# Layer 1's attention heads: in each step the last head's context tile stands in front of this head's scores instead of behind them

## The reference

```python
q = _rope((x @ Wq).reshape(N, t, H, DQ).transpose(0, 2, 1, 3))   # H = 16
k = _rope((x @ Wk).reshape(N, t, G, DQ).transpose(0, 2, 1, 3))   # G = 4, each used by 4 heads
scores = (q @ k.T + alibi) / sqrt(DQ)
scores = 30.0 * tanh(scores / 30.0)
probs = softmax(where(causal, scores, -inf))
ctx = probs @ v
out = ctx.reshape(N, t, H * DV) @ Wo + bo
```

## Time and profile before

| | us |
|---|---|
| three timed runs | 852.80, 853.99, 854.36 |
| their median | 853.99 |
| profiled execution | 852.75 |
| its span, first to last instruction | 850.9 |
| PE busy | 783.5 (92% of the span) |
| DVE busy | 609.0 (72%) |
| ACT busy | 465.7 (55%) |
| POOL busy | 422.4 (50%) |

### The profile page before, as it was taken

One profiled execution on the slowest core, in us unless ns is written; L12 is line 12 of the kernel. 1 busy time (PEld: TensorE's weight loads), 2 busy tenths in 40 slices (PEclk: granted clock), 3 DMA queues, 4 the chain that ended last, 5 costly groups with the idle time before them and its releaser, 6 DMA issues.

```text
span 850.9 us, 13950 instructions
## 1 busy us (share of the span) xinstructions
PE 783.5 (92%) x4871; PEld 637.8 (75%) x4871; DVE 609.0 (72%) x1077; ACT 465.7 (55%) x822; POOL 422.4 (50%) x479
## 2 busy tenths in 40 slices
PE   7999999978788878899998999999999997989996
PEld 6776776754233257698998989989999997978884
DVE  7588868457999867878788877997777543445455
ACT  4433342278888733686855565556665724555431
POOL 1767827333555445456444534576656514555530
PEclk9999999997999899999999999999999999999999
DMA  5211194000000040000000000010101599444107
GB/s 183 75 38 37 38 304 126 1 1 1 1 1 2 1 127 27 25 7 25 7 19 7 27 7 7 26 44 32 39 32 46 210 244 382 132 124 112 46 11 237
DMA packets 50115, 59.81 MB, mean 70 GB/s; under 512 B 13559, under 2 KB 41084, under 8 KB 50048
## 3 DMA queue, kind: packets, MB, share of 16 engines
q1 hardware_dynamic: 45488, 50.49, 19.2%
q0 software_dynamic: 4560, 8.44, 2.8%
HBM read 41.11 MB, written 21.86 MB: 74 GB/s over the span
## 4 chain that ended last, share of the span: by engine, by line
PE 58%; DVE 8%; POOL 6%; ACT 6%; issue 4%; DMA 3%; POOLq 0%; ACTq 0%; DVEq 0%; SPq 0%
PE ps L786 12%; PE ps L516 9%; PE ps L518 8%; PE ps L517 8%; PE ps L879 4%; PE ps L876 3%; PE ps L910 3%; POOL A L1777 2%; DMA xa<-xg_scratch 2%; PE ps L613 2%; PE ps L698 2%; PE ps L558 2%; PE ps L858 1%; DVE cap L1477 1%; PE ps L795 1%
## 5 line engine op out<-in xcount | busy, mean ns | idle before, releaser
L786 PE MATMUL ps<-V,P 128*128 128x129 f32 x1152 | 150.7, 276 | 0.0
L1131 ACT ACTIVATE cap<-cap 128x1024 f32<-128x1024 f32 (+7 forms) x128 | 87.1, 680 | 110.3 <-DVE cap L1477 106.6
L786 PEld LDWEIGHTS ps<-V,P 128*128 128x128 f32 x1152 | 143.3, 192 | 2.7
L1477 DVE SCALAR_TENSOR_TENSOR cap<-dist,ps 128x1024 f32<-128x1024 f32 (+7 forms) x128 | 95.3, 750 | 28.7 <-PE ps L518 20.8
L1701 POOL TENSOR_SCALAR_AFFINE_SELECT P<-P 128x128 f32<-128x128 f32 x128 | 38.3, 299 | 143.7 <-ACT P L1136 143.3
L1833 POOL DMA_INDIRECT y_scratch<-y_sb,aux_s x63 | 62.1, 985 | 70.8 <-ACT y_sb L1176 40.3
L1136 ACT ACTIVATE P<-cap 128x1024 f32<-128x1024 f32 (+7 forms) x128 | 87.6, 685 | 4.1
L516 PE MATMUL ps<-q_hi,k_hi 128*128 128x512 f32 x192 | 71.8, 374 | 6.4 <-DVE cap L1477 5.0
L518 PE MATMUL ps<-q_lo,k_hi 128*128 128x512 f32 x192 | 67.0, 349 | 0.0
L517 PE MATMUL ps<-q_hi,k_lo 128*128 128x512 f32 x192 | 66.7, 347 | 0.0
L1629 DVE TENSOR_SCALAR gu<-ps 128x256 f32<-128x256 f32 (+1 forms) x63 | 28.9, 458 | 47.6 <-PE ps L876 16.8
(11 more groups left out here) (288 smaller groups left out, 2104.7 us busy)
## 6 DMA issues: line engine op xcount, KB each, us to landing
xg_scratch<-blank SPq DMA_DIRECT2D x1, 8127.0 KB, 31.1
xa<-xg_scratch SPq DMA_DIRECT2D x63, 128.0 KB
ew<-in_experts SPq DMA_DIRECT2D x3, 1920.0 KB, 12.3
y<-y_scratch SPq DMA_DIRECT2D x8, 512.0 KB, 5.8
pk<-in_packed SPq DMA_DIRECT2D x8, 384.0 KB, 3.1
pks<-in_scales SPq DMA_DIRECT2D x8, 384.0 KB, 4.1
ew<-in_experts SPq DMA_DIRECT2D x1, 3072.0 KB, 17.5
wqk<-in_wqk SPq DMA_DIRECT2D x20, 128.0 KB, 2.0
```

Source lines behind the costliest of these rows:

```text
L786: last = pe.matmul(ps[:, 4 + r % 2, o:o + D1 + 1], P1[:, h % 2, a:a + P], V1[:, j, h // REP, :], start=(j == 0), stop=(j == t))
L1131: act.activation(cap[:, n % 2, 0:w], cap[:, n % 2, 0:w], ACT.Tanh, scale=1.0 / (CAP * float(D1) ** 0.5))\
L1477: dve.scalar_tensor_tensor(out=cap[:, n % 2, 0:w], in0=dist[:, 0:w], scalar=slope, in1=psf[:, 1024 * (n % 2):1024 * (n % 2) + w], op0=ALU. ...
```

## The change

Two statements of `schedule()` change places. C(h-1, j) now stands in front of S(h, j), for h = 1 to 15; head 0 has no context to put there, and behind head 15 come contexts alone.

```diff
         for j in range(NT):
+            if h >= 1:
+                steps.append(("context", h - 1, j))
             if h < H1:
                 steps.append(("scores", h, j))
-            if h >= 1:
-                steps.append(("context", h - 1, j))
```

## The result

Before 852.80 us, after 858.93 us (medians of 19 runs each, timed in turn on one chip). The ratio is not the quotient of the two medians, which is 1.0072 and lies in its interval; one run after, 868.61 us, was in a slower state of the chip and does not count in the ratio. I had forecast 855.1 us, with a range of 852.4 to 858.2. The change costs 6 to 7 us where I had summed up 1.1.

The account below looks back on a forecast made before the run. PE, busy 92% of the span, was taken as the bound, its standstills deciding. Terms 1.1 - 0.8 + 0.6 + 0.2 = +1.1 us, on the median 853.99, gave 855.1 us; range 852.4 to 858.2.

Parts of the forecast that it names:

- The frame: Whole kernel: PE busy 92% of the span; what counts is when PE stands still and whether what ends it moves.
- Part 1: Matmuls of the 15 heads: same work in another order, put at nothing, with 1.2 us either way in the range.
- Part 2: Head 7, second T: S(7,4) ends one C later, so T starts 1.11 us later and waits 2.6 us; +1.1 us.
- Part 3: Heads 2 and 3: waits at S(2,7) and S(3,0) go, that at S(3,4) stays; first P of head 3 earlier, -0.8 us.
- Part 4, head 5: Head 5: wait at S(5,7) moves into P's; read-out of 0.68 us against ACT's 0.40 to spare delays P, +0.3 us.
- Part 4, head 9: Head 9: S(9,7)'s 1.25 us bring nothing; bias of j = 2 later by a read-out, carried to P, +0.3 us.
- are safe by the same reckoning: Other starts of a head: PE still has 2.3 us of work between S(h-1,6) and S(h,0), so no loss was expected.
- The sign that I had named for being wrong: First P of heads 6 and 10 sooner than before, or waits over 0.3 us at S(h,0) of other heads.
- The rival of the clock: Behind longer holes in head 7 and ahead of head 6's first P, clock falls: 1.65 us each, 856.8 or 858.4; chance 0.27.
- Part 5: End of heads: S(15,0) later by C(14,0), +0.2 us; wait for sorted rows ends 43.1 us after the last send.

Follow-up runs that it names:

- old_but_h7: Kernel before the change, with C(6,4) put ahead of S(7,4) in that one step alone; ratio to before 1.0023 (1.0002 to 1.0044).

## Why the prediction was wrong, point by point

- **The frame was right**: what counts is where PE stands still. The three single swaps of heads 7, 9 and 10 timed at 1.0023, 1.0016 and 1.0035; together +0.0074, each of them known to about 0.002, while the whole change gave +0.0081. So the price of the change is that of one step in head 7 and of heads 9 and 10; what head 8 adds and what the others gain, 0.7 and 0.9 us of shift, about cancel.
- **Part 1** (matmuls at nothing): right; between the losing places, in head 8 and from head 12 on, the shift stays constant within 0.3 us.
- **Part 2** (head 7, +1.1): right, also in old_but_h7.
- **Part 3** (heads 2 and 3, -0.8): the total over heads 1 to 6 came out as -0.6, but at P of head 3 it is only -0.2, and 0.16 of that stood already at the second P of head 1. So heads 2 and 3 gave nothing up to that P; the same holds within 0.05 us in all eleven profiled kernels that have the new order there. The gain came behind it, where the wait of S(3,4) went, which I had said would stay: -0.19 at the P ahead of S(3,4), -0.62 at the next. That the total fits the forecast of parts 3 and 4 (-0.5) is luck. S(3,0) waited 1.51 us. The term was mis-sized by one row that I had taken over at its old length, L1521 (0.42 us), between bias 5 and `cT_lo`. After:

```profile
395.49 1.50 DVE L1521 TENSOR_TENSOR scr<-scr 128x256 f32<-128x256 f32 x1
397.03 0.69 DVE L1498 TENSOR_TENSOR cT_lo<-ps,cT_hi 128x512 fp32r<-128x512 f32 x1
397.64 0.41 DVE L1477 SCALAR_TENSOR_TENSOR cap<-dist,ps 128x256 f32<-128x256 f32 x1
```

  My time for bias 6, 394.8, lies 2.8 us behind the `cT_lo` of the earlier trace rows. That `cT_lo` is now at 393.75, so bias 6 was due at 396.55 and came 1.09 us later, which is L1521's stretch (1.50 - 0.42). It ran into POOL's `wo_lo`, 395.43 to 396.71. The match is close. L1521 takes 1.5 us in the kernels with the new order in head 2 and 0.42 us in those with the old, but no run moved it away to see what S(3,0) does then.
- **Part 4, head 5** (+0.3): measured 0.0; P of head 6 stayed behind the addition of O, as said. POOL took up the delay: ahead of the second `q_lo` it idled 0.24 us instead of 0.50, and its `wqk_lo` and rotation behind it took 0.74 and 1.34 us instead of 0.83 and 1.45. That P waited 1.55, not 2 us, since part of the wait stood at an O before it (0.70).
- **Part 4, head 9** (+0.3): this term failed in size, 1.3 us of waits. I charged one read-out of 0.68 us against 0.38 of slack that ACT had; but the delay goes through POOL's mask and send, where none of it was taken up, and two read-outs move in: the one ahead of bias 2 in head 9, and the last of head 8. With either of them gone 0.7 are left, with both 0.
- **The sentence that the other starts of a head "are safe by the same reckoning"**, in the paragraph of the sum, is the step whose failure cost most: 2.6 us of waits in heads 10 and 11, 4.1 with the clock. The sign that I had named for being wrong, a wait of over 0.3 us at S(h,0) of another head, is in the trace, 0.92 us at S(11,0). I had worked out for head 7 that a C of 1.11 us ahead of S(h,4) delays the chain bias, router pair, `cT_lo`. The same chain stands in head 10, with a larger pair behind the bias, and I neither looked for the chain elsewhere nor asked what POOL does while it runs. The delay is 1.11 us; the pair's stretch makes 3.46 more.
- **The rival of the clock** was no rival but a part of the outcome, and I gave it 0.27; the sum carried it at nothing, and it cost 4.1 us. Its price per fall was about right (1.65 forecast; 1.5, 1.1 and 1.5 measured). Its number was not: three falls, not up to two, and none ahead of P of head 6. What I held against it, that the clock stayed at 1.00 behind the 2.6 us ahead of L558, was one draw. Up to that place all the kernels are the same, and in or just behind the same 2.58 us of standstill the clock fell in ten of the 18 profiled ones. In after, where that wait ended at 178.32:

```profile
180.50:182.50 2.00, 2.00 (x11) 2.00 (x11) 0.69 (x1) 1.97 (x4) 0.50 (x1) 0.50 0.00 0
```

- **Part 5** (+0.2): the last heads gained 0.3. The expert stage's wait is tied to the last send as said: 688.97 to 731.17, 42.2 us (43.1 forecast):

```profile
731.17 0.50 PE L858 MATMUL ps<-ident,xa 128*128 128x128 f32 x2 [3.82 <-DMA xa<-xg_scratch]
```

## What to carry to other kernels

When a reordering delays one chain, look for every place where that chain stands, not only for those where the engine already waits: a place without a wait can have less slack than the delay. And don't take durations over to a new time: a DVE operation with two SBUF inputs keeps its length only as long as what POOL does beside it is the same. The places where a reordering loses can be found with a condition on the list of steps, one run each, and the order kept where it gains.

## What the runs showed of the hardware that I had not expected

- **Two-input DVE operations beside POOL's.** L1597 (128x256) took 0.42 to 3.94 us and L1600 (128x512) 0.69 to 2.60 us, by what POOL did; POOL's own operations in the heads grew by less than 0.5 us each (`wqk_lo` from 0.74 to 0.92 us in after, 1.20 in old_but_h7), and it made no difference that the DVE operation had begun first (583.80 against 584.20 in head 10 of after). Beside an indirect DMA alone the pair was not stretched (it is POOL's issue that took 1.22 instead of 0.99 us). Whether it costs anything is another question: nothing for 3.9 us in head 9, nothing for 1.75 us more in head 10, and 2.8 us for 3.46 more together with the swap's own delay.
- **The clock behind a standstill is a matter of chance at 2.0 and 2.6 us.** Behind the same 1.98 us of head 0, unfilled in 14 profiled kernels, the sum of the windows below 1.00 gives 3.4 us at the lower level in seven, 6.8 us in five and none in two. Behind the 2.58 us ahead of L558, or at their end, it fell in ten of 18, behind 2.59 us in head 7 in six of seven; behind 1.48 us there in none of ten. In the pairs of waits it fell in five of seven for 1.15 + 0.92 or 1.15 + 1.19 us in head 10, and in five of seven for 1.04 to 1.59 us, alone or with 0.77 behind, in head 9 in the new order (behind the 1.25 to 1.80 us of the old order in none of eleven). Filled, none of five fell. So several runs are needed before a fall is called a cost or a cure. It may be one reason why the runs of one kernel spread over 3 to 12 us. The time ahead of S(0,0) varies by 6 us as well; its cause stays open.
